# A fused cross-attention, self-attention and gated low-rank layer: all engines' instruction order and the load order redone

## The chip, the cores and the metric

The kernel runs on one NeuronCore of a Trainium2 chip, in one launch. The metric is the time of one execution on the device in microseconds (us); lower is better. PE is TensorE (matrix products and transposes), ACT is ScalarE, DVE is VectorE, POOL is GpSimd, and SP is the engine that here only issues the DMA loads and stores.

## The reference, cut to what matters

```
x: (16, 32, 512)   ctx: (16, 512, 512)          # all float32
q1 = fake_quant(layernorm(x)); q2 = fake_quant(ctx)      # round to 8 bits, scale back
x  = x + q1 @ q2                                         # per batch element
h  = layernorm(x)
q, k, v = h @ wq.T + bq, h @ wk.T + bk, h @ wv.T + bv    # 32 heads of 16 channels
x  = x + softmax over heads(q k^T / 4) v                 # per token: 32x32 scores between heads
h  = layernorm(x)
gate = softmax of the 16 largest of 64 scores (h @ Wq.T @ keys.T)
x  = x + ((h @ A.T) * gate) @ B.T * 2
```

The attention is between the 32 heads of one token, not between tokens. The 512 tokens are the 16 batch elements times 32 rows.

## The kernel before, in words

**Tiles.** The 512 tokens are four tiles of 128 tokens (`TILES` = 4), and each tile holds four batch elements (`BPT` = 4). Each batch element has its own context matrix, 512 by 512 in float32, 1 MiB. The sixteen contexts are called c0 to c15: c0 to c3 belong to tile 0, c4 to c7 to tile 1, c8 to c11 to tile 2, c12 to c15 to tile 3.

**A context's way.** SP loads it into one of four `raw` slots (`load_ctx`, L262 to L269; from c4 on it first waits until the context four before it has been quantised). ACT quantises it to 8 bits in `cu8` (`quantise_ctx`, L408 to L423). POOL, or DVE for c2 and c3, subtracts 128 and writes bfloat16 into `cbf` (`center_ctx`, L330 and L615). PE multiplies it with the tile's quantised rows (`product(t, first, end)`, L970 to L985), whose results lie in `ps1`. c3 is loaded and quantised in two halves.

**A tile's way.** (1) `norm_stats`, `norm_1`, `quantise_x`, `center_q1`, `transpose_q1`, `copy_q1T`. (2) four `product`s, `finish_product`, `transpose_y1`, `residual_1`. `shift_x` adds a row term to x before that. (3) Second norm (`norm_2_stats`, then `norm_2` on DVE for tiles 0 and 1, `apply_norm_2` on ACT for tiles 2 and 3), `transpose_h2`, `copy_h2T`. (4) Three projections with wq, wk, wv (`project_q`, `project_k`, `project_v`; `first` and `second` are the two halves of the contraction), biases added on DVE, `spread_heads` (two long DVE transposes, of q and of k). (5) `scores(t, 0)` and `scores(t, 1)`, 64 small products each; `softmax_shift`, `exp_scores`, `transpose_probs`. `place_v` copies v into a block-diagonal tile with four ACT copies. `context(t)` is 64 more small products. (6) `transpose_context`, `residual_2`, third norm, `transpose_h3`, `router_scores`, `choose_experts`, `exp_gates`, `gates`, `bottleneck` (with wa), `gate_z`, `transpose_zg`, `copy_zgT`, `output` (with wb), `residual_3`, store.

**What sets the order.** Each engine's program is a list of such calls written out by hand, and each engine runs its list strictly in order, with a wait on a semaphore wherever it needs another engine's result. So an instruction that waits holds back everything behind it on its engine. Work of four tiles is interleaved in the lists: products of tile t+1 stand between the projections and the attention of tile t. SP's list is an order too: a load that waits for a slot holds back the loads behind it. c12 and c13 are issued after `scores_done` has reached 3, that is after `scores(1, 0)` (L292), and c14 and c15 after `scores(1, 1)` (L295).

**Fillers.** `keep_busy(3)` (L1170) and `keep_clock_up(n)` (L1176) are matmuls whose results nobody reads; they keep TensorE active in places where it would wait.

**Biases.** The three bias rows are spread over 128 partitions by three matmuls with a matrix of ones (`spread_biases`), copied out by ACT (`copy_bias`).

**Router weights.** `transpose_router_weights`, `combine_router_weights` and ACT's `copy_router_weights` run once, between tile 0's v projection and tile 1's q projection, which reuses their PSUM bank and so waits for that copy.

Of the kernel before, what the change touches and what calls it, by code (L numbers as in the profile page):

```python
# [18 lines left out]
S = Q // 2  # L19
# [12 lines left out]
def build(nc, x, ctx, quant_in, biases_in, wqT, wkT, wvT, aT, bT, wrT, keysT, out):  # L32
# [13 lines left out]
    with ExitStack() as stack:  # L46
# [214 lines left out]
        def _(sp):  # L261
# [31 lines left out]
            load_ctx(3 * BPT)  # L293
            load_ctx(3 * BPT + 1)
            sp.wait_ge(sem_scores_done, 4)  # L295
            load_ctx(3 * BPT + 2)
            load_ctx(3 * BPT + 3)
# [11 lines left out]
        def _(pool):  # L309
# [57 lines left out]
            for padded in (q_sb, k_sb):  # L367
                nc.gpsimd.memset(padded[:, D:], 0.0).then_inc(sem_q_pad, 1)
# [3 lines left out]
            rsqrt(1, 0, sem_ln2_mean, sem_ln2_eps, sem_ln2_rstd)  # L372
            pool.wait_ge(sem_h2_ready, 1)
            center_ctx(BPT)
            center_ctx(BPT + 1)
            finish_norm_1(2)
            finish_norm_1(3)
            center_ctx(BPT + 2)
            center_ctx(BPT + 3)
            rsqrt(1, 1, sem_ln2_mean, sem_ln2_eps, sem_ln2_rstd)  # L380
            pool.wait_ge(sem_h2_ready, 2)
            for n in range(2 * BPT, 3 * BPT):
                center_ctx(n)
            for u in range(1, TILES):
                residual_2(u - 1)
                finish_norm_3(u - 1)
                if u == 2:
                    for n in range(3 * BPT + 1, NB):
                        center_ctx(n)
                if u + 1 < TILES:  # L390
                    finish_norm_2(u + 1)
                if u == 1:
                    center_ctx(3 * BPT)
# [4 lines left out]
        def _(act):  # L398
# [145 lines left out]
            shift_x(2)  # L544
            quantise_x(3)
# [3 lines left out]
            quantise_ctx(3 * BPT)  # L549
            apply_norm_2(2)  # L550
# [3 lines left out]
            copy_zgT(0)  # L554
            copy_h2T(2)
            copy_q1T(3)
            shift_x(3)
            quantise_ctx(3 * BPT + 1)
            quantise_ctx(3 * BPT + 2)
            for u in range(2, TILES):  # L560
                apply_norm_3(u - 1)
                if u == 2:
                    quantise_ctx(3 * BPT + 3)
                copy_h3T(u - 1)
                exp_scores(u, 0)
                place_v(u)
                exp_scores(u, 1)
                exp_gates(u - 1)
                copy_zgT(u - 1)
                if u + 1 < TILES:  # L570
                    apply_norm_2(u + 1)
                    copy_h2T(u + 1)
# [6 lines left out]
        def _(dve):  # L579
# [280 lines left out]
            row_sum_term(1)  # L860
            dve.wait_ge(sem_x_rest_in, 16)
            norm_stats(x_sb[:, 2, :], 0, 2, sem_ln1_stats, sem_ln1_mean)
            norm_stats(x_sb[:, 3, :], 0, 3, sem_ln1_stats, sem_ln1_mean)
            bias_q(0)
            norm_1(2)
            spread_heads(qT, q_sb, sem_q_biased, sem_qT_ready, 0)
            bias_k(0)
            spread_heads(kT, k_sb, sem_k_biased, sem_kT_ready, 0)
            finish_product(1)
            residual_1(1)  # L870
# [3 lines left out]
            bias_v(0)  # L874
            transpose_probs(0, 0)
            center_q1(2)
            row_sum_term(2)
            transpose_v(0)
# [5 lines left out]
            bias_k(1)  # L884
            transpose_context(0)
            spread_heads(kT, k_sb, sem_k_biased, sem_kT_ready, 1)
            finish_product(2)
            norm_3(0)
            softmax_shift(1, 0)
            residual_1(2)  # L890
            norm_2_stats(2)
            bias_v(1)
            transpose_probs(1, 0)
            softmax_shift(1, 1)
            transpose_v(1)
            transpose_probs(1, 1)
            choose_experts(0)
            gates(0)
            gate_z(0)
            sum_gates(0)  # L900
            center_q1(3)
            row_sum_term(3)
# [411 lines left out]
```

## Time and profile before

| | us |
|---|---|
| median of 3 runs | 147.32 |
| lowest and highest of them | 145.54, 147.86 |
| the profiled execution: its own time | 144.67 |
| the span inside it that the profile covers | 142.9 |
| PE busy | 117.8 (82%) |
| DVE busy | 93.5 (65%) |
| ACT busy | 71.2 (50%) |
| POOL busy | 47.1 (33%) |

Everything below counts from the start of the 142.9 us span. The remaining 1.77 us of the execution's own time lie around the span. Busy shares are averages over the whole span; the stages have different limits, so they don't say by themselves what a change is worth. The matmul record's length overlaps with the next one's, so the distance from one start to the next is shorter than the length shown.

### The profile page before, as it was taken

The numbers are of one execution on the slowest core, as the hardware profiler recorded it, in microseconds if no ns is written. First come the engines' busy times: TensorE is split into PE (matmuls) and PEld (weight loads), VectorE is DVE, ScalarE is ACT, GpSimd is POOL, SyncE is SP. The second block draws the span as 40 slices with busy tenths as digits, with TensorE's granted clock in tenths as the row PEclk, the third lists the DMA queues.
The fourth block names the chain that finished last, engine by engine and source line by source line (L and its number), as shares of the span: only waits on it lengthen the run. The fifth ranks groups of instructions, "written<-read, shape, count | busy, mean of one in ns | idle before, by whom it ended". The sixth has DMA issues, their size and how long they took to land.

```text
span 142.9 us, 4282 instructions
## 1 busy us (share of the span) xinstructions
PE 117.8 (82%) x1864; PEld 70.6 (49%) x1864; DVE 93.5 (65%) x189; ACT 71.2 (50%) x87; POOL 47.1 (33%) x61
## 2 busy tenths in 40 slices
PE   0029657992898999989599999999999799899992
PEld 0024343432566447657155445965444376446881
DVE  5740696417579988699582377799347759893512
ACT  0369976559356999038923991372302115411120
POOL 4018225259507553923407575000830000002000
PEclk9999999999999999999999999999999999999999
DMA  2899999999999920079920100000010000000102
GB/s 63 314 421 419 392 406 403 420 403 382 423 420 384 388 81 5 0 310 381 388 108 5 73 2 0 5 5 5 0 73 2 0 5 5 5 0 21 52 5 73
DMA packets 7093, 24.44 MB, mean 171 GB/s; under 512 B 1185, under 2 KB 1441, under 8 KB 5154
## 3 DMA queue, kind: packets, MB, share of 16 engines
q1 hardware_dynamic: 6928, 24.16, 43.3%
q8 instruction: 15, 0.25, 0.7%
q14 instruction: 4, 0.03, 0.1%
q10 hardware_dynamic: 146, 0.01, 0.1%
HBM read 23.11 MB, written 1.05 MB: 169 GB/s over the span
## 4 chain that ended last, share of the span: by engine, by line
PE 55%; DMA 17%; ACT 11%; DVE 8%; issue 5%; POOL 1%; SPq 0%; DVEq 0%; ACTq 0%
PE ps_b L1042 19%; PE ps_a L1042 14%; DMA wv<-in_L_attn_wv_dram 13%; PE ps_att L1111 5%; ACT cu L422 4%; DMA raw<-in_ctx_dram 4%; PE ps L982 3%; PE ps_att L1122 3%; PE ps_att L1145 2%; ACT v_diag L440 2%; PE ps_t L1023 1%; PE ps L1097 1%; DVE v_diag L839 1%; PE ps_b L1164 1%; PE ps_a L1164 1%
## 5 line engine op out<-in xcount | busy, mean ns | idle before, releaser
L422 ACT ACTIVATE cu<-raw,sc_in,sc_recip 128x2048 uint8<-128x2048 f32 x15 | 30.9, 2088 | 6.4 <-DMA raw<-in_ctx_dram 6.3
L336 POOL TENSOR_SCALAR cbf<-cu 128x2048 bf16<-128x2048 uint8 x14 | 26.6, 1903 | 18.6 <-ACT cu L422 16.8
L324 POOL TENSOR_SCALAR var_eps<-mean_var 128x1 f32<-128x1 f32 x12 | 2.7, 223 | 55.8 <-DVE mean_var L583 55.7
L982 PE MATMUL ps<-q1T,cbf 128*128 128x33 bf16 x256 | 7.9, 178 | 4.5 <-POOL cbf L336 2.8
L440 ACT COPY v_diag<-vT 32x512 f32<-32x512 f32 x16 | 10.1, 633 | 2.4 <-DVE vT L704 2.1
L1111 PE MATMUL ps_att<-kT,qT 16*32 16x32 f32 x1024 | 10.5, 193 | 0.9 <-issue 0.7
L982 PEld LDWEIGHTS ps<-q1T,cbf 128*128 128x128 bf16 x256 | 7.3, 96 | 7.3 <-POOL cbf L336 3.5
L447 ACT ACTIVATE probs<-probs 128x512 f32<-128x512 f32 x8 | 5.0, 627 | 11.7 <-DVE probs L712 11.7
L1111 PEld LDWEIGHTS ps_att<-kT,qT 16*32 16x32 f32 x1024 | 9.6, 104 | 1.9 <-issue 1.7
L581 DVE BATCH_NORM_STATS2 stats<-x_sb 128x6 f32<-128x512 f32 x12 | 8.2, 686 | 2.1 <-DMA x_sb<-in_x_dram 1.3
L959 PE MATMUL ps_t<-ident_bf,q 128*128 128x128 bf16 x12 | 1.4, 248 | 10.0 <-DVE q L606 10.0
L459 ACT COPY h3T<-ps_t 128x256 f32<-128x256 f32 x8 | 2.6, 375 | 13.6 <-PE ps_t L1023 13.6
L587 DVE TENSOR_SCALAR h<-x_sb,mean_var,rstd 128x512 f32<-128x512 f32 x7 | 4.9, 693 | 5.9 <-POOL rstd L327 5.8
L696 DVE STREAM_TRANSPOSE qT<-q_sb 128x1024 f32<-128x1024 f32 x4 | 7.8, 1958 | 0.3
L696 DVE STREAM_TRANSPOSE kT<-k_sb 128x1024 f32<-128x1024 f32 x4 | 7.8, 1946 | 0.3
L1042 PE MATMUL ps_b<-wb,zgT 128*128 128x512 f32 x16 | 7.6, 606 | 0.5 <-ACT zgT L459 0.5
L1042 PE MATMUL ps_a<-wq,h2T 128*128 128x512 f32 x16 | 7.4, 602 | 0.7 <-ACT h2T L429 0.7
L1042 PE MATMUL ps_b<-wv,h2T 128*128 128x512 f32 x16 | 7.8, 610 | 0.0
L1042 PE MATMUL ps_a<-wv,h2T 128*128 128x512 f32 x16 | 7.5, 599 | 0.3 <-DMA wv<-in_L_attn_wv_dram 0.3
L327 POOL TENSOR_TENSOR rstd<-var_eps,minus_half 128x1 f32<-128x1 f32 x12 | 7.1, 588 | 1.0
L1042 PE MATMUL ps_a<-wa,h3T 128*128 128x512 f32 x16 | 7.4, 602 | 0.0
L1042 PE MATMUL ps_a<-wk,h2T 128*128 128x512 f32 x16 | 7.3, 595 | 0.0
(135 smaller groups left out, 222.3 us busy)
## 6 DMA issues: line engine op xcount, KB each, us to landing
raw<-in_ctx_dram SPq DMA_DIRECT2D x15, 1024.0 KB, 10.7
raw<-in_ctx_dram SPq DMA_DIRECT2D x2, 512.0 KB, 11.8
wq<-in_L_attn_wq_dram SPq DMA_DIRECT2D x1, 1024.0 KB, 14.0
wk<-in_L_attn_wk_dram SPq DMA_DIRECT2D x1, 1024.0 KB, 12.4
wv<-in_L_attn_wv_dram SPq DMA_DIRECT2D x1, 1024.0 KB, 19.0
wa<-in_L_ffn_A_w_dram SPq DMA_DIRECT2D x1, 1024.0 KB, 13.1
wb<-in_L_ffn_B_w_dram SPq DMA_DIRECT2D x1, 1024.0 KB, 15.5
out_dram<-x_sb SPq DMA_DIRECT2D x3, 256.0 KB, 2.0
```

The source lines that it names most:

```text
L327: nc.gpsimd.tensor_tensor(rstd[:, norm, t:t + 1], var_eps[:, norm, t:t + 1], minus_half[:, :], ALU.pow).then_inc(rstd_sem, 1)
L336: nc.gpsimd.tensor_scalar(cbf[:, n % BF_SLOTS, :, :], cu8[:, n % U8_SLOTS, :], -CENTER, 1.0, ALU.add, ALU.mult).then_inc(sem_ctx_bf_pool, 1)
L422: nc.scalar.activation(cu8[:, n % U8_SLOTS, :], raw[:, n % RAW_SLOTS, :], ACT.Identity, bias=sc_in[:, 3:4], scale=sc_recip[:, 2:3]).then_i ...
L440: nc.scalar.copy(v_diag[rows, :, g, 0:HD], vT[rows, :, :])\
L447: nc.scalar.activation(probs[:, half, :], probs[:, half, :], ACT.Exp, scale=HD ** -0.5).then_inc(sem_s_exp, 1)
L581: nc.vector.bn_stats(stats[:, norm, t, :], src).then_inc(stats_sem, 1)
L587: nc.vector.tensor_scalar(dst, src, mean_var[:, norm, t, 0:1], rstd[:, norm, t:t + 1], ALU.subtract, ALU.mult).then_inc(done_sem, 1)
L696: nc.vector.transpose(dst[:, :, :].rearrange("p i h -> p h i"), view(src[:, :], 0, [[HD, H], [1, Q]])).then_inc(done, 1)
L982: last = nc.tensor.matmul(ps1[:, m // 2, col:col + LW], cbf[:, n % BF_SLOTS, c, m * P:(m + 1) * P], q1T[:, t, c, b, :], start=(c == 0), st ...
L1042: last = nc.tensor.matmul(dst[:, :], aT[:, c, :], w[:, c, :], start=(c == 0), stop=(c == KC - 1))
L1111: last = nc.tensor.matmul(ps_att[Q * j:Q * j + H, i, :], qT[rows, i, :], kT[rows, i, :], start=True, stop=True)
L1122: last = nc.tensor.matmul(view(ps_att[Q * j:Q * (j + 1), 0, :], BPT * H * i, [[1, BPT * (HD + 1)]]), eT[:, token, :], v_diag[:, token, :, ...
```

## The change

It changes no instruction's work but one filler's operands. It changes the order of the calls in the lists of all five engines. In short:

- SP: c4 is issued directly behind c3, ahead of the second tile's x, the rest of x and wq; c5 comes before wk; c11 comes behind wa and wb.
- ACT: `shift_x(0)` moves up behind c0's quantisation, c4's quantisation ahead of the bias copies, `copy_h2T(1)` ahead of `copy_router_weights`, `place_v(0)` ahead of `copy_q1T(2)`, `apply_norm_2(2)` from behind c12's quantisation to behind `copy_zgT(0)`.
- PE: the biases first of all; half of `project_k(0)` behind two products of tile 1; the first product of tile 2 ahead of `context(0)` and the last product of tile 2, `product(2, 3, 4)`, ahead of `project_v(1, first)` instead of behind it; fillers moved.
- DVE and POOL: the same kind of exchanges, written out.

```diff
@@ sync (SP) @@
             load_x(0, 1, sem_x_in)
-            for n in range(BPT):
-                load_ctx(n)
+            load_ctx(0)
+            load_ctx(1)
+            load_ctx(2)
+            load_ctx(3)
+            load_ctx(4)
             load_x(1, 2, sem_x1_in)
+            load_x(2, 4, sem_x_rest_in)
             sp.dma_start(wq[:, :, :], chunked(wqT)).then_inc(sem_wq_in, 16)
-            load_ctx(BPT)
+            load_ctx(5)
             sp.dma_start(wk[:, :, :], chunked(wkT)).then_inc(sem_wk_in, 16)
-            load_x(2, TILES, sem_x_rest_in)
-            load_ctx(BPT + 1)
-            load_ctx(BPT + 2)
-            load_ctx(BPT + 3)
+            load_ctx(6)
+            load_ctx(7)
             sp.dma_start(wv[:, :, :], chunked(wvT)).then_inc(sem_wv_in, 16)
...
-            for n in range(2 * BPT, 3 * BPT):
-                load_ctx(n)
+            load_ctx(8)
+            load_ctx(9)
+            load_ctx(10)
             sp.dma_start(wa[:, :, :], chunked(aT)).then_inc(sem_a_in, 16)
             sp.dma_start(wb[:, :, :], chunked(bT)).then_inc(sem_b_in, 16)
+            load_ctx(11)
             sp.wait_ge(sem_scores_done, 3)
@@ scalar (ACT) @@
             quantise_x(0)
-            for n in range(BPT):
-                quantise_ctx(n)
-            for i in range(3):
-                copy_bias(i)
+            quantise_ctx(0)
             shift_x(0)
+            quantise_ctx(1)
+            quantise_ctx(2)
+            quantise_ctx(3)
+            quantise_ctx(4)
+            copy_bias(0)
+            copy_bias(1)
+            copy_bias(2)
             quantise_x(1)
-            quantise_ctx(BPT)
+            copy_q1T(1)
             copy_h2T(0)
-            copy_q1T(1)
+            quantise_ctx(5)
+            quantise_ctx(6)
+            quantise_ctx(7)
             shift_x(1)
-            for n in range(BPT + 1, 2 * BPT):
-                quantise_ctx(n)
             quantise_x(2)
-            quantise_ctx(2 * BPT)
+            quantise_ctx(8)
             copy_router_rows()
             exp_scores(0, 0)
+            copy_h2T(1)
             copy_router_weights()
-            copy_h2T(1)
-            quantise_ctx(2 * BPT + 1)
-            quantise_ctx(2 * BPT + 2)
+            quantise_ctx(9)
+            quantise_ctx(10)
             exp_scores(0, 1)
+            place_v(0)
             copy_q1T(2)
-            place_v(0)
-            quantise_ctx(2 * BPT + 3)
+            quantise_ctx(11)
+            quantise_x(3)
             shift_x(2)
-            quantise_x(3)
             exp_scores(1, 0)
             apply_norm_3(0)
             copy_h3T(0)
-            quantise_ctx(3 * BPT)
-            apply_norm_2(2)
+            quantise_ctx(12)
             exp_scores(1, 1)
             place_v(1)
             exp_gates(0)
             copy_zgT(0)
+            apply_norm_2(2)
             copy_h2T(2)
...
@@ vector (DVE) @@
             center_ctx(3)
+            finish_product(0)
             dve.wait_ge(sem_x1_in, 16)
             norm_stats(x_sb[:, 1, :], 0, 1, sem_ln1_stats, sem_ln1_mean)
-            finish_product(0)
+            residual_1(0)
             norm_1(1)
-            residual_1(0)
...
             softmax_shift(0, 1)
-            norm_1(3)
-            transpose_probs(0, 1)
             bias_q(1)
             spread_heads(qT, q_sb, sem_q_biased, sem_qT_ready, 1)
+            transpose_probs(0, 1)
...
+            gates(2)
+            sum_gates(2)
+            gate_z(2)
@@ tensor (PE) @@
             def keep_busy(count):
                 for _ in range(count):
-                    nc.tensor.matmul(ps_att[:, S:, :].rearrange("p i h -> p (i h)"), ident[:, :], h1[:, 0, :],
+                    nc.tensor.matmul(ps_att[:, S:, :].rearrange("p i h -> p (i h)"), ones[:, :], bias_rows[:, 0:D],
                                      start=True, stop=True)
...
+            spread_biases()
             transpose_q1(0)
-            spread_biases()
...
             project_k(0, first)
-            project_k(0, second)
             product(1, 0, 1)
             product(1, 1, 2)
+            project_k(0, second)
             product(1, 2, 3)
             project_v(0, first)
             product(1, 3, 4)
...
             project_k(1, second)
+            product(2, 0, 1)
             context(0)
-            product(2, 0, 1)
             product(2, 1, 2)
             product(2, 2, 3)
+            product(2, 3, 4)
             project_v(1, first)
-            product(2, 3, 4)
             scores(1, 0)
...
             transpose_h3(0)
-            keep_clock_up(3)
             router_scores(0)
             bottleneck(0, first)
             bottleneck(0, second)
+            keep_clock_up(3)
             context(1)
...
             product(3, 2, 3)
+            router_scores(1)
             product(3, 3, 4)
-            router_scores(1)
             scores(2, 1)
+            transpose_y1(3)
             bottleneck(1, first)
-            transpose_y1(3)
             bottleneck(1, second)
...
             output(2, first)
+            keep_clock_up(5)
             output(2, second)
-            keep_clock_up(5)
```

## Rows read from the trace of the kernel before

**Rows 1.** The page: the chain that ended last, share of the span by engine.

```profile
PE 55%; DMA 17%; ACT 11%; DVE 8%; issue 5%; POOL 1%; SPq 0%; DVEq 0%; ACTq 0%
```

**Rows 2.** By stretch: length, busy PE, PEld, DVE, ACT, POOL, granted clock, DMA share, GB/s.

```profile
0.00:36.86 36.86, 19.69 (x156) 10.60 (x156) 20.57 (x43) 23.88 (x20) 15.85 (x28) 1.00 0.94 364
36.86:60.08 23.22, 22.55 (x581) 14.28 (x581) 19.09 (x29) 15.17 (x16) 11.83 (x9) 1.00 0.62 241
60.08:73.53 13.45, 11.22 (x231) 7.16 (x231) 10.68 (x27) 8.55 (x14) 4.47 (x8) 1.00 0.78 315
73.53:99.80 26.27, 26.02 (x452) 15.23 (x452) 18.39 (x38) 13.94 (x19) 9.39 (x8) 1.00 0.04 13
```

**Rows 3.** The chain of waits in order of time: start, length, what.

```profile
17.82 19.00 DMA wv<-in_L_attn_wv_dram
...
60.09 5.43 DMA raw<-in_ctx_dram
...
67.55 0.80 ACT h L513
68.35 0.52 ACT probs L447
...
71.42 1.15 PE ps_att L1122 x64
```

**Rows 4.** SP's issues in order of time: start, length, what.

```profile
11.21 0.33 SPq L269 DMA_DIRECT2D raw<-in_ctx_dram  x1
...
37.02 0.51 SPq L291 DMA_DIRECT2D wb<-in_L_ffn_B_w_dram  x1
```

**Rows 5.** Loads by size, us to landing: c3's second half (issued 3.23), then wb.

```profile
raw<-in_ctx_dram SPq DMA_DIRECT2D x1, 512.0 KB, 12.1
...
wb<-in_L_ffn_B_w_dram SPq DMA_DIRECT2D x1, 1024.0 KB, 15.5
```

**Rows 6.** PE's timeline: start, length, what, and what ended the idle time before.

```profile
25.25 3.70 PE L1042 MATMUL ps_a<-wq,h2T 128*128 128x512 f32 x8 [0.68 <-ACT h2T L429]
...
35.96 0.57 PE L982 MATMUL ps<-q1T,cbf 128*128 128x33 bf16 x16 [2.79 <-POOL cbf L336]
...
56.43 1.96 PE L1042 MATMUL ps_b<-wv,h2T 128*128 128x512 f32 x4
58.23 0.56 PE L982 MATMUL ps<-q1T,cbf 128*128 128x33 bf16 x16
58.73 1.33 PE L1111 MATMUL ps_att<-kT,qT 16*32 16x32 f32 x128
```

**Rows 7.** The bias matmuls: duration min/median/max in ns, first and last start.

```profile
L967 PE MATMUL ps_a<-bias_rows,ones x2: 1061/1112/1163, 10.4 to 11.4; 128*128 128x512 f32 x2
...
L967 PE MATMUL ps_att<-bias_rows,ones x2: 593/692/791, 13.9 to 14.5; 128*128 128x512 f32 x2
```

**Rows 8.** ACT's timeline.

```profile
18.75 0.73 ACT L506 ACTIVATE x_sb<-x_sb,row_term 128x512 f32<-128x512 f32 x1
...
45.01 0.37 ACT L476 COPY wr_keys<-ps_b 128x256 f32<-128x256 f32 x1 [0.26 <-PE ps_b L1089]
...
53.79 2.09 ACT L422 ACTIVATE cu<-raw,sc_in,sc_recip 128x2048 uint8<-128x2048 f32 x1
```

**Rows 9.** POOL's timeline.

```profile
55.96 1.90 POOL L336 TENSOR_SCALAR cbf<-cu 128x2048 bf16<-128x2048 uint8 x1 [3.77 <-ACT cu L422]
```

**Rows 10.** DVE's timeline.

```profile
18.07 0.68 DVE L581 BATCH_NORM_STATS2 stats<-x_sb 128x6 f32<-128x512 f32 x1
18.79 0.18 DVE L583 BATCH_NORM_AGGREGATE mean_var<-stats 128x2 f32<-128x6 f32 x1
...
50.72 0.71 DVE L722 STREAM_TRANSPOSE eT<-probs 128x512 f32<-128x512 f32 x1 [0.28 <-ACT probs L447]
51.36 0.65 DVE L672 TENSOR_TENSOR q_sb<-ps_b,biases 128x512 f32<-128x512 f32 x1
52.11 1.95 DVE L696 STREAM_TRANSPOSE qT<-q_sb 128x1024 f32<-128x1024 f32 x1
```

More of the change, by code:

```diff
@@ L372, in _ @@
             rsqrt(1, 0, sem_ln2_mean, sem_ln2_eps, sem_ln2_rstd)
+            finish_norm_1(2)
             pool.wait_ge(sem_h2_ready, 1)
[L374 to L376 removed]
+            center_ctx(4)
+            center_ctx(5)
+            for padded in (q_sb, k_sb):
+                nc.gpsimd.memset(padded[:, D:], 0.0).then_inc(sem_q_pad, 1)
+            center_ctx(6)
+            center_ctx(7)
             finish_norm_1(3)
[L378 to L379 removed]
             rsqrt(1, 1, sem_ln2_mean, sem_ln2_eps, sem_ln2_rstd)
             pool.wait_ge(sem_h2_ready, 2)
[L382 to L393, printed above, removed]
+            center_ctx(8)
+            center_ctx(9)
+            center_ctx(10)
+            center_ctx(11)
+            residual_2(0)
+            finish_norm_3(0)
+            finish_norm_2(2)
+            residual_2(1)
+            center_ctx(12)
+            center_ctx(13)
+            finish_norm_3(1)
+            center_ctx(14)
+            center_ctx(15)
+            finish_norm_2(3)
+            residual_2(2)
+            finish_norm_3(2)
             rsqrt(2, TILES - 1, sem_ln3_mean, sem_ln3_eps, sem_ln3_rstd)
@@ L554, in _ @@
             copy_zgT(0)
+            apply_norm_2(2)
             copy_h2T(2)
+            shift_x(3)
+            quantise_ctx(13)
+            quantise_ctx(14)
             copy_q1T(3)
[L557 to L572, printed above, removed]
+            apply_norm_3(1)
+            quantise_ctx(15)
+            copy_h3T(1)
+            place_v(2)
+            exp_scores(2, 0)
+            exp_scores(2, 1)
+            exp_gates(1)
+            copy_zgT(1)
+            apply_norm_2(3)
+            copy_h2T(3)
+            apply_norm_3(2)
+            copy_h3T(2)
+            exp_scores(3, 0)
+            place_v(3)
+            exp_scores(3, 1)
+            exp_gates(2)
+            copy_zgT(2)
             copy_h3T(TILES - 1)
@@ L899, in _ @@
             gate_z(0)
+            transpose_context(1)
             sum_gates(0)
-            center_q1(3)
-            row_sum_term(3)
-            for u in range(2, TILES):
-                transpose_context(u - 1)
-                residual_3(u - 2)
-                norm_3(u - 1)
-                bias_q(u)
-                spread_heads(qT, q_sb, sem_q_biased, sem_qT_ready, u)
-                bias_k(u)
-                spread_heads(kT, k_sb, sem_k_biased, sem_kT_ready, u)
-                if u + 1 < TILES:
-                    bias_v(u)
-                    softmax_shift(u, 0)
-                else:
-                    softmax_shift(u, 0)
-                    bias_v(u)
-                transpose_v(u)
-                if u + 1 < TILES:
-                    finish_product(u + 1)
-                transpose_probs(u, 0)
-                softmax_shift(u, 1)
-                choose_experts(u - 1)
-                transpose_probs(u, 1)
-                if u + 1 < TILES:
-                    residual_1(u + 1)
-                gates(u - 1)
-                gate_z(u - 1)
-                if u + 1 < TILES:
-                    norm_2_stats(u + 1)
-                sum_gates(u - 1)
+            residual_3(0)
+            norm_3(1)
+            bias_q(2)
+            spread_heads(qT, q_sb, sem_q_biased, sem_qT_ready, 2)
+            bias_k(2)
+            spread_heads(kT, k_sb, sem_k_biased, sem_kT_ready, 2)
+            bias_v(2)
+            transpose_v(2)
+            softmax_shift(2, 0)
+            finish_product(3)
+            transpose_probs(2, 0)
+            softmax_shift(2, 1)
+            choose_experts(1)
+            residual_1(3)
+            gates(1)
+            transpose_probs(2, 1)
+            gate_z(1)
+            norm_2_stats(3)
+            transpose_context(2)
+            sum_gates(1)
+            residual_3(1)
+            norm_3(2)
+            bias_q(3)
+            spread_heads(qT, q_sb, sem_q_biased, sem_qT_ready, 3)
+            bias_k(3)
+            spread_heads(kT, k_sb, sem_k_biased, sem_kT_ready, 3)
+            softmax_shift(3, 0)
+            bias_v(3)
+            transpose_v(3)
+            transpose_probs(3, 0)
+            softmax_shift(3, 1)
+            choose_experts(2)
+            transpose_probs(3, 1)
+            gates(2)
+            sum_gates(2)
+            gate_z(2)
             t = TILES - 1
@@ L1232, in _ @@
             output(0, second)
+            project_q(2, first)
             transpose_q1(3)
-            project_q(2, first)
             project_q(2, second)
```

27 lines of the change are left out of this document (14 added, 13 removed).

## The prediction

> **What bounds the kernel now.** I read the chain of waits first. PE holds 55% of it, DMA 17% [rows 1], so this is a kernel in which PE works nearly all the time, with some places where it waits. The table by stretch shows where. Until 36.86 us PE is busy for only 19.69 us, while the DMA engines are at a share of 0.94 [rows 2]. The chain crosses this stretch on one load: wv, issued at 17.82, lands at 36.82 [rows 3]. What PE does before that has room. From 36.86 to 60.08 PE is busy 22.55 of 23.22 us: PE is the bound. From 60.08 to 73.53 it is busy only 11.22 of 13.45, and from 73.53 to 99.80 again 26.02 of 26.27 [rows 2]. In the weak stretch the chain is: the load of c12, which may only be issued once `scores(1, 0)` is done, 5.43 us to landing, its quantisation on ACT, then on ACT `apply_norm_2(2)` at 67.55, `exp_scores(1, 1)` at 68.35, `place_v(1)`, and only then `context(1)` at 71.42 [rows 3]. So three things set the end: when wv lands, how soon after it `scores(1, 0)` ends, and what stands on ACT between c12 and `place_v(1)`.
>
> **Loads up to wv.** The new order has the same loads ahead of wv: 12 MiB with wv. Nothing is taken out, so wv can only land earlier or later if the queue runs dry or runs at another pace. Dry: c4 waits for c0's quantisation and is issued at 11.21 [rows 4], and now x1, the rest of x and wq stand behind it. At that moment what is queued lasts until c3's second half lands, 3.23 + 12.1 = 15.3 [rows 5], so 4.1 us. A MiB landed 5.43 us after its issue with an idle DMA [rows 3]; its own transfer takes about 2.6 (the six loads behind wv take from 36.82 to wb's landing at 37.02 + 15.5 = 52.5 [rows 3 to 5]), which leaves 2.8 us of delay, less than 4.1. The queue does not run dry. Pace: between 15.3 and 36.82 lie 7.75 MiB, 2.8 us each. At that pace the new order lands c4 at 18.1, x1 at 18.8, wq at 23.0, c5 at 25.8, wk at 28.5, wv at 36.8. I take 0 for wv; the ends are -1.3 (if the 7.75 MiB ran at 2.6) and +1.3 (as much the other way, since no row bounds it).
>
> **Work before 36.86.** `shift_x(0)` ahead of c1 delays the later contexts of tile 0 by its 0.73 us [rows 8], and the statistics of x1, 0.68 + 0.18 [rows 10], now stand between `finish_product(0)` and `residual_1(0)`. At most 1.6 us together: `project_q(0)` goes from 25.25 [rows 6] to 26.85 at the latest, after wq's 23.0. It takes 3.7, the first half of K 1.85 (wk is there), two products 1.14, the second half of K 1.85: 35.4. The next product waited for POOL until 35.96 before [rows 6] and will again. The first half of `project_v` needs wv at 36.82. So the delay is hidden, with 36.82 - 0.57 - 35.4 = 0.8 us to spare; without that cover it would cost its 1.6. c4 earlier, the exchanged K half and the bias copies are worth 0 for the same reason: the load of wv ends last.
>
> **Tile 1 to tile 2: product(2, 3) pulled ahead.** Before, PE went from three products of tile 2 to `project_v(1, first)` at 56.43, then to `product(2, 3)` at 58.23, then `scores(1, 0)` at 58.73 [rows 6]. The product's operand, c11 centred, was ready at 55.96 + 1.90 = 57.86 [rows 9], only 0.37 before PE came for it. The projection was the cover of that work. Now the product stands first: PE comes for it at 56.43 and waits, because PE's queue lets nothing pass. ACT reaches c11 no sooner. Its list up to there holds the same calls (c9, c10, an exp, the four v copies, q1T), and it began c11 at 53.79 [rows 8] without waiting; since `copy_router_weights` (0.37 [rows 8]), which filled a wait for `transpose_h2(1)`, now stands behind that wait, c11 comes 0.37 later: quantised from 54.16, centred at 58.23. PE: product from 58.23, v half from 58.73 for 1.80 (58.23 - 56.43), `scores(1, 0)` from 60.53. **+1.80 us.** Bounds: +1.4 if ACT regains the 0.37, +2.3 if POOL or ACT lose half a microsecond more.
>
> c11's load, now behind wa and wb, lands last of the same six: 52.5, 1.6 us before ACT wants it at 54.16. Cost 0. `copy_h2T(1)` and the router copy still end just before `project_q(1)` needs them, 0 to +0.3.
>
> On DVE, `bias_q(1)` and the long transpose of q now stand ahead of `transpose_probs(0, 1)`: 50.72 + 0.65 + 1.95 + 0.71 [rows 10] = 54.0. `context(0)` stands behind `product(2, 0)` now; with its 1.15 [rows 3] and two products of 0.57 to go until 56.43 it starts near 54.1. Cost 0, with a tenth to spare, +0.3 at most. k's transpose ends sooner and is not late next.
>
> **c12 and place_v(1).** c12 and c13 wait for `scores(1, 0)` and so are issued, and land, 1.80 later (the queue is empty, the 5.43 stay). ACT quantises c12 at once. Then `apply_norm_2(2)` no longer stands ahead of the exp: 68.35 - 67.55 = **-0.80 us** [rows 3] for `place_v(1)`, `context(1)`, `exp_gates(0)`, the gating and `output(0)`. What it does now, behind `copy_zgT(0)`, is needed by `transpose_h2(2)` behind half of `output(0)`, 1.8 us later: 0.80 fits. The filler moved from before the router to the wait before `context(1)` is worth 0, since PE still reaches `context(1)` early.
>
> **From 73.53 on** PE has no gap worth naming until 99.80 [rows 2], and the exchanges keep the sum of each chain: `gates(1)` before `transpose_probs(2, 1)` delays `context(2)` by about half a microsecond, but the second norm of tile 3 (statistics, POOL, ACT) ended last there and has the same work ahead of it. `place_v(2)` ahead of `exp_scores(2, 0)` is covered by `finish_product(3)` on DVE. `residual_2(1)` on POOL now goes ahead of c12 and c13, which are needed only after the scores of tile 2. `sum_gates(2)` before `gate_z(2)` and the fillers between the halves of `output(2)` sit beside `context(3)` and the third norm. 0, with -0.5 and +0.5 as ends.
>
> **Sum:** 1.80 - 0.80 = **+1.0 us**. The profiled execution's own time is 144.67 (span 142.9): 145.7. That execution lay 2.65 us below the median of the runs, 147.32; on the median the sum gives **148.3**. The ends of all terms added give about -0.9 and +3.0 on top of the median.
>
> **Rivals.**
>
> *A. The wait at product(2, 3) does not come* (ACT or POOL get to c11 1.8 us earlier). Only the -0.8 is left: 146.5. For it speaks only that 23 us of ACT's list are reshuffled there; against it, that ACT began c11 without waiting and with only 0.37 us of room. Chance 0.12.
>
> *B. The loads run faster in the new order.* wv lands up to 1.3 earlier and the whole chain shifts: 148.3 - 1.3 = 147.0. For it: 2.8 against 2.6 us per MiB in two parts of the same trace. Against: same bytes and sizes. Chance 0.12, and 0.06 more for a gain beyond 2%, several of these together.
>
> *C. Slower: TensorE turns slow in the front part.* The first bias matmuls took 1061 ns, one of the last 593 [rows 7], the same shape: at first PE runs at half pace (the rows' granted clock says 1.00 [rows 2] and does not show it), after nothing at all. Now the biases run before the first transposes, and PE then waits for c0's centring and has only short bursts of products until the fillers. If PE falls back to half pace, six filler matmuls cost 0.47 each, 2.8 us, and the eight of `project_q(0)` up to 3.8 more. It decides once it exceeds the 0.8 us of room before wv: +2.0 with the fillers alone, 150.3; up to +5.8 with q, 154. Against it: in the old order a gap of 2.79 us before 35.96 was followed by 1.96 us for four wide matmuls, no slower than elsewhere [rows 6]. Chance 0.12.
>
> The Trainium skill, "TensorE: Matmul & The Clock Gate", Part 1, says that the half-rate clock is the default state, that sustained activity releases it, and that an idle stretch brings it back. By that rule an earlier warm-up followed by a wait is wasted, which speaks against moving the biases; the trace agrees in its slow first matmuls (1061 ns), and shows no fall after the gap of 2.79 us.
>
> *D. The loads come later.* wv lands 1.3 late, or c11, last of its six, more than 1.6 late, and the PE chain behind it shifts with the excess; with the stall that makes 3 us or more: 150.3 and over. Only the changed queue speaks for it. Chance 0.08.
>
> *The forecast itself*, +1.0 within about -0.5 and +1.5 around it: chance 0.50.
>
> **How the numbers follow.** About 2% (2.9 us) is what can be told from no change. Forecast, A, B and half of C lie within it: 0.50 + 0.12 + 0.12 + 0.06 = 0.80. Beyond it upward are the other half of C and D, 0.14; downward the 0.06 named under B. The range takes the terms' ends on the median, 146.4 to 150.3, and since the runs before alone went from 145.54 to 147.86, it reaches down to 145.4.
>
> **What would show it.** Right: wv lands at 36.8 give or take 0.5; PE idle about 1.8 us before the 16 small matmuls of `product(2, 3)`, ended by POOL's cbf; `scores(1, 0)` 1.8 later than before; the c12 load again in the chain; no h (`apply_norm_2`) between c12's quantisation and the exp; `context(1)` near 72.4; the end of the span near 143.9. Wrong: PE idle elsewhere between 36.8 and 56, filler matmuls of 1061 ns, or `output(0)` earlier than 73.5.

## The result and the profile after

The changed kernel takes 147.45 us (median of 20 runs, 146.80 to 149.27); the kernel before, run between them, 147.24 (20 runs, 144.32 to 148.84). The comparison of the undisturbed runs gives a ratio of 1.015 [1.011, 1.019]; it is above the ratio of the medians, 1.001, because it compares with the lower part of the runs before. The forecast was 148.3 (145.4 to 150.3), within 2% of no change: both hold.

The profiled execution after: 147.5 us of its own, span 145.7, against 144.67 and 142.9. That is +2.8, where the forecast made it +1.0. From the page of the changed kernel: the engines' busy time, the granted clock of TensorE (PE) in 40 slices (tenths), and the chain's shares.

```profile
PE 122.4 (84%) x1864; PEld 72.4 (50%) x1864; DVE 93.2 (64%) x189; ACT 70.9 (49%) x87; POOL 46.6 (32%) x61
...
PEclk9999956999999999599999999999999999999999
...
PE 50%; DMA 16%; ACT 16%; issue 7%; DVE 7%; POOL 2%; SPq 0%; ACTq 0%; DVEq 0%
```

PE's busy time rose by 4.6 us with the same 1864 matmuls, and the clock row has two dips, at a seventh and at four tenths of the span. The page before shows none (its row is all 9, and its stretches say 1.00 [rows 2]). ACT's share of the chain rose from 11 to 16% [rows 1]. The same stretches as in [rows 2], cut at the same events (wv has landed, c12 is issued behind `scores(1, 0)`, `output(0)` begins, `output(1)` begins):

```profile
0.00:36.94 36.94, 22.43 (x156) 11.73 (x156) 21.54 (x43) 23.74 (x20) 16.07 (x26) 0.91 0.94 365
36.94:63.54 26.60, 24.34 (x581) 14.76 (x581) 18.66 (x31) 15.07 (x16) 12.81 (x13) 0.94 0.53 208
63.54:76.16 12.62, 11.41 (x231) 7.33 (x231) 10.66 (x26) 7.85 (x13) 1.05 (x3) 1.00 0.83 332
76.16:103.17 27.01, 26.11 (x452) 15.34 (x452) 18.22 (x37) 14.64 (x20) 11.88 (x11) 1.00 0.04 14
```

The first stretch is as long as before. The second took 26.60 instead of 23.22, at a mean clock below 1.00: +3.4. The third took 12.62 instead of 13.45: 0.8 is given back. `output(0)` begins at 76.16, before at 73.53: +2.6. `output(1)` is 3.4 later than 99.80: `context(2)` ahead of it begins at 101.01, behind a wait of 0.60 for DVE's transpose of the probabilities, where before it began at 97.76 without one. By the end it is +2.8. The chain after, in order of time (start, length, what; the rows answer to [rows 3]):

```profile
18.43 18.51 DMA wv<-in_L_attn_wv_dram
...
63.55 5.31 DMA raw<-in_ctx_dram
...
74.05 1.16 PE ps_att L1147 x64
```

wv lands at 36.94 (36.82 before); the load of c12 is in the chain again; no h stands between it and probs (ACT's rows are shown further down). PE's timeline after, answering to [rows 6]:

```profile
21.48 4.18 PE L1198 MATMUL ps_att<-bias_rows,ones 128*128 128x512 f32 x6
...
27.04 3.70 PE L1067 MATMUL ps_a<-wq,h2T 128*128 128x512 f32 x8 [0.72 <-ACT h2T L437]
...
36.98 1.98 PE L1067 MATMUL ps_a<-wv,h2T 128*128 128x512 f32 x4 [1.52 <-DMA wv<-in_L_attn_wv_dram]
...
46.83 3.70 PE L1067 MATMUL ps_b<-wq,h2T 128*128 128x512 f32 x8
...
58.33 0.62 PE L1007 MATMUL ps<-q1T,cbf 128*128 128x33 bf16 x16 [1.55 <-POOL cbf L340]
58.79 3.51 PE L1067 MATMUL ps_b<-wv,h2T 128*128 128x512 f32 x4
62.23 0.95 PE L1136 MATMUL ps_att<-kT,qT 16*32 16x32 f32 x90
```

PE stands before `product(2, 3)` for 1.55 us, ended by POOL's cbf, as forecast. What was not forecast is the next row: the same four wide matmuls of `project_v(1, first)` that took 1.96 before [rows 6] take 3.51. PE by stretch (length, busy, granted clock, DMA share, GB/s) tells why:

```profile
54.70:56.80 2.10, 2.08 (x100) 1.00 0.00 0
56.80:58.33 1.53, 0.00 (x0) 1.00 0.00 0
58.33:58.79 0.46, 0.46 (x17) 0.69 0.00 0
58.79:60.50 1.71, 1.71 (x8) 0.50 0.04 10
```

The granted clock is 1.00 through the wait, falls within the 16 small matmuls behind it (0.69 on average) and is 0.50, the level of 1.2 GHz, from 58.79 on. POOL centres c11 from 56.38, as before it did from 55.96 [rows 9]:

```profile
56.38 1.90 POOL L340 TENSOR_SCALAR cbf<-cu 128x2048 bf16<-128x2048 uint8 x1 [3.85 <-ACT cu L430]
```

### The profile page after: what moved, and what is told of

It is laid out like the page before. It is cut to its first block, busy times and chain, and to the rows that moved or that the text cites. A ratio compares the mean times of both kernels' runs of the same rounds, so it can differ in the third digit from the quotient of the medians.

```text
span 145.7 us, 4282 instructions
## 1 busy us (share of the span) xinstructions
PE 122.4 (84%) x1864; PEld 72.4 (50%) x1864; DVE 93.2 (64%) x189; ACT 70.9 (49%) x87; POOL 46.6 (32%) x61
## 3 DMA queue, kind: packets, MB, share of 16 engines
HBM read 23.11 MB, written 1.05 MB: 166 GB/s over the span
## 4 chain that ended last, share of the span: by engine, by line
PE 50%; DMA 16%; ACT 16%; issue 7%; DVE 7%; POOL 2%; SPq 0%; ACTq 0%; DVEq 0%
PE ps_b L1067 17%; DMA wv<-in_L_attn_wv_dram 13%; PE ps_a L1067 12%; ACT cu L430 7%; PE ps_att L1136 4%; DMA raw<-in_ctx_dram 4%; ACT v_diag L448 3%; PE ps_att L1147 3%; PE ps_att L1170 2%; PE ps L1007 2%; PE ps_t L1048 2%; PE ps L1122 1%; POOL cbf L340 1%; DVE v_diag L855 1%; DVE eT L738 1%
## 5 line engine op out<-in xcount | busy, mean ns | idle before, releaser
L1007 PE MATMUL ps<-q1T,cbf 128*128 128x33 bf16 x256 | 8.5, 179 | 4.4 <-POOL cbf L340 2.0
L1067 PE MATMUL ps_b<-wv,h2T 128*128 128x512 f32 x16 | 9.4, 716 | 0.0
L992 PE MATMUL ps_a<-bias_rows,ones 128*128 128x512 f32 x2 | 2.1, 1138 | 8.3 <-DMA bias_rows<-in_biases_dram 8.3
L1067 PE MATMUL ps_b<-wk,h2T 128*128 128x512 f32 x16 | 7.4, 597 | 0.0
L726 DVE TENSOR_REDUCE s_max<-ps_att 128x16 f32<-128x512 f32 x8 | 5.4, 669 | 3.1 <-PE ps_att L1136 3.1
L1067 PE MATMUL ps_b<-wq,h2T 128*128 128x512 f32 x16 | 7.3, 599 | 0.0
```

What stands on the lines that cost most here:

```text
L726: nc.vector.tensor_reduce(s_max[:, half], ps_att[:, half, :], AX_X, ALU.max).then_inc(sem_s_max, 1)
L1007: last = nc.tensor.matmul(ps1[:, m // 2, col:col + LW], cbf[:, n % BF_SLOTS, c, m * P:(m + 1) * P], q1T[:, t, c, b, :], start=(c == 0), st ...
L1067: last = nc.tensor.matmul(dst[:, :], aT[:, c, :], w[:, c, :], start=(c == 0), stop=(c == KC - 1))
```

## The experiments

The question was twofold: what makes the V half slow, and why the medians are nearly equal when the profiled executions differ by 2.8. My theory for the first: the wait itself brings PE to half clock, and without it the V half takes 1.96. Rival: the slowness belongs to the changed order as such and stays without the wait. For the second: the kernel before usually loses in other places what its one profiled execution did not lose.

**The V half put back ahead of the product, in the changed kernel.**

```diff
             product(2, 2, 3)
-            product(2, 3, 4)
             project_v(1, first)
+            product(2, 3, 4)
             scores(1, 0)
```

> The changed kernel with one pair put back: project_v(1, first) ahead of product(2, 3) again. Theory 1 (the product pulled ahead makes PE idle for 1.5 us, and that idle time brings TensorE's clock down to half for the next 3.4 us, which costs another 1.6): both go, the four wide matmuls of project_v(1, first) take 1.96 us instead of 3.51, scores(1, 0) starts near 58.8 instead of 62.2, span 142.1 to 142.7 against 145.7. Rival 1 (the clock falls near 58.8 whatever PE does just before, because of the busy share of the whole stretch or of the front part): only the wait goes, the four matmuls still take about 3.5 us, span 143.9 to 144.2.

Measured: 147.36 (10 runs; the kernel before beside it 146.53, 19 runs), ratio 1.008 [1.003, 1.013]. PE's timeline of it:

```profile
46.65 5.39 PE L1067 MATMUL ps_b<-wq,h2T 128*128 128x512 f32 x8
...
57.98 1.96 PE L1067 MATMUL ps_b<-wv,h2T 128*128 128x512 f32 x4
```

The wait is gone and the V half is at 1.96 again. But `project_q(1)` took 5.39 instead of 3.70, at half clock, and so in part did the router and the bottleneck behind it (1.81 and 4.65 instead of 1.10 and 3.65). So the local part of the theory holds, but the expected span of 142.1 to 142.7 did not come: this execution's was 145.6. The move itself can't have caused the fall at `project_q(1)`, since PE's list is that of the changed kernel up to `product(2, 2, 3)`, which stands behind it, and the changed kernel took 3.70 there. Against the kernel before, the ratio is 0.7% lower than that of the changed kernel (1.015), but the intervals overlap: a gain of the move is not shown.

**The wait filled.** Seven `keep_clock_up` matmuls ahead of the product, everything else as changed.

```diff
             product(2, 2, 3)
+            keep_clock_up(7)
             product(2, 3, 4)
```

> The changed kernel with seven filler matmuls (0.22 us each) ahead of product(2, 3), so that PE waits no longer idle. Theory 1: the wait stays (product(2, 3) still starts near 58.3), but the clock stays at full level and project_v(1, first) takes 1.96 us: span 145.7 - 1.6 = 144.1, at most 144.4. Rival 1: the clock falls all the same, span 145.7 to 145.9.

Measured: 146.99 (4 runs), 1.011 [1.002, 1.021], span 144.6, 0.2 above the highest that was expected.

```profile
47.18 3.70 PE L1067 MATMUL ps_b<-wq,h2T 128*128 128x512 f32 x8
...
56.98 1.81 PE L1204 MATMUL ps<-ident 128*128 128x128 f32 x14
58.68 0.57 PE L1007 MATMUL ps<-q1T,cbf 128*128 128x33 bf16 x16
59.10 1.96 PE L1067 MATMUL ps_b<-wv,h2T 128*128 128x512 f32 x4
```

The order and the product's place in time are those of the changed kernel, only PE is not idle, and the V half takes 1.96 (wv landed 0.35 later in this execution, and all behind it with it). This isolates the cause: the idle time ahead of the product, not the order. It is one profiled execution, but the others agree: over all fourteen kernels of this document, the two with the wait (this change and the next experiment) have these four matmuls at 3.5, the twelve without it at 1.96.

**Only that exchange, in the kernel before.**

```diff
             product(2, 2, 3)
-            project_v(1, first)
             product(2, 3, 4)
+            project_v(1, first)
             scores(1, 0)
```

> The kernel before with one pair exchanged: product(2, 3) ahead of project_v(1, first), nothing else. Theory 1: PE idles 1.4 us before the product, then the half clock: scores(1, 0) near 61.9 to 62.2 instead of 58.7, and without the move of apply_norm_2(2) nothing is given back: span 142.9 + 1.6 + 1.5 = 146.0, 145.7 to 146.4. Rival 1 (the fall needs the rest of the change): 144.3 to 144.7, the wait alone.

Measured: 150.36 (4 runs), 1.019 [1.010, 1.029], span 147.0, above the 146.4 expected.

```profile
58.02 0.58 PE L982 MATMUL ps<-q1T,cbf 128*128 128x33 bf16 x16 [1.16 <-POOL cbf L336]
58.45 3.50 PE L1042 MATMUL ps_b<-wv,h2T 128*128 128x512 f32 x4
61.88 1.38 PE L1111 MATMUL ps_att<-kT,qT 16*32 16x32 f32 x128
```

The exchange alone brings the wait, the half clock and `scores(1, 0)` 3.15 later than 58.73 [rows 6]: 1.5 of wait and late product, 1.6 of clock. The span is longer by 4.1, not 3.15: `context(1)` comes 2.8 later, and the clock falls once more behind its wait of 1.74, so that the first four matmuls of `output(0)` take 3.41 instead of 1.98.

**Only `apply_norm_2(2)` moved, in the kernel before.**

```diff
             quantise_ctx(3 * BPT)
-            apply_norm_2(2)
             exp_scores(1, 1)
...
             copy_zgT(0)
+            apply_norm_2(2)
             copy_h2T(2)
```

> The kernel before with ACT's apply_norm_2(2) moved from behind the quantisation of c12 to behind copy_zgT(0), nothing else. Theory: place_v(1), context(1) and output(0) start 0.8 us earlier: span 142.1. Rival: another wait takes its place (transposed gating on DVE, or transpose_h2(2) waiting for the norm behind output(0, first)), span 142.6 to 142.9.

Measured: 145.57 (10 runs), 0.996 [0.990, 1.002], span 143.5, and the lowest of its spans 142.2. First ACT's timeline of it, then PE's, then the row of the kernel before for the same `context(1)`:

```profile
66.99 2.10 ACT L422 ACTIVATE cu<-raw,sc_in,sc_recip 128x2048 uint8<-128x2048 f32 x1
68.99 0.61 ACT L447 ACTIVATE probs<-probs 128x512 f32<-128x512 f32 x1
```

```profile
20.83 3.75 PE L1173 MATMUL ps_att<-h,ident 128*128 128x512 f32 x6
...
36.08 0.57 PE L982 MATMUL ps<-q1T,cbf 128*128 128x33 bf16 x16 [2.22 <-POOL cbf L336]
36.82 3.51 PE L1042 MATMUL ps_a<-wv,h2T 128*128 128x512 f32 x4 [0.18 <-DMA wv<-in_L_attn_wv_dram]
...
72.15 1.15 PE L1122 MATMUL ps_att<-v_diag,eT 128*32 128x68 f32 x64 [0.75 <-ACT v_diag L440]
```

```profile
71.42 1.15 PE L1122 MATMUL ps_att<-v_diag,eT 128*32 128x68 f32 x64 [1.50 <-ACT v_diag L440]
```

The exp follows the quantisation directly, and the wait before `context(1)` fell from 1.5 to 0.75: the -0.8. But in this execution `project_v(0, first)`, whose place and code are those of the kernel before, took 3.51 instead of 1.98, behind a gap of 2.22 at the place where the kernel before had 2.79. So the gap that did no harm in the profiled execution before does harm in another.

**Only K's second half moved behind two products**, which shortens that gap, in the kernel before.

```diff
             project_k(0, first)
-            project_k(0, second)
             product(1, 0, 1)
             product(1, 1, 2)
+            project_k(0, second)
             product(1, 2, 3)
```

> The kernel before with one pair exchanged on PE: the second half of project_k(0) behind the first two products of tile 1, nothing else. Theory 2 (in most executions of the kernel before, PE's idle 2.2 to 3.0 us ahead of product(1, 2) bring the clock down, and project_v(0, first) behind wv's landing takes 3.51 instead of 1.98; the change closes that gap in part, which is what it gives back): the idle time is cut in two, project_v(0, first) takes 1.98 us, the lowest time stays near 144.5 and the median falls by 0.5 to 1.5 us. Rival 2 (the spread of the kernel before comes from elsewhere): same times as before.

Measured: 145.61 (10 runs; before 147.41, 17 runs), 0.996 [0.989, 1.004].

```profile
36.40 0.57 PE L982 MATMUL ps<-q1T,cbf 128*128 128x33 bf16 x16 [1.05 <-POOL cbf L336]
37.33 1.98 PE L1042 MATMUL ps_a<-wv,h2T 128*128 128x512 f32 x4 [0.36 <-DMA wv<-in_L_attn_wv_dram]
```

The gap is 1.05 and the V half runs at full pace, in the one profiled execution. The median is 1.8 lower, the interval includes no change: alone it is not shown to pay.

**The gap filled instead**, with 22 recorded matmuls more, in the kernel before.

```diff
             product(1, 1, 2)
+            keep_clock_up(11)
             product(1, 2, 3)
```

> The kernel before with eleven filler matmuls ahead of product(1, 2, 3), where PE waits for c6, nothing else. Theory 2: no half clock at project_v(0, first), lowest time as before (144.3 to 144.7), median lower by 1 to 1.5 us (145.1 to 145.6 where the kernel before has 146.5). Rival 2: no change.

Measured: 159.44 (4 runs), 1.090 [1.074, 1.107]. No theory expected that. `project_v(0, first)` is at full pace, but later:

```profile
46.49 1.24 PE L1111 MATMUL ps_att<-kT,qT 16*32 16x32 f32 x122
51.95 0.33 PE L1111 MATMUL ps_att<-kT,qT 16*32 16x32 f32 x6 [4.22 <-issue]
52.20 3.69 PE L1042 MATMUL ps_b<-wq,h2T 128*128 128x512 f32 x4
...
103.28 0.18 PE L1111 MATMUL ps_att<-kT,qT 16*32 16x32 f32 x1 [2.04 <-issue]
...
133.10 0.25 PE L1111 MATMUL ps_att<-kT,qT 16*32 16x32 f32 x5 [2.06 <-issue]
```

PE stops inside a run of identical small matmuls, with no semaphore to wait for, and is at half clock behind the stop (four wide matmuls in 3.69).

**Two more with fillers.** One was the single move of `apply_norm_2(2)` with fillers at three gaps (11, 3 and 3 calls); the other the changed kernel, V half put back (not shown in the cut), with three calls at each of three gaps:

```diff
             project_k(0, second)
+            keep_clock_up(3)
             product(1, 2, 3)
...
             transpose_router_weights()
+            keep_clock_up(3)
             combine_router_weights()
...
             transpose_h3(0)
+            keep_clock_up(3)
             router_scores(0)
```

> The kernel before with apply_norm_2(2) moved behind copy_zgT(0) and fillers where PE waits idle: eleven ahead of product(1, 2, 3), three between the two router weight steps, three ahead of context(1). The sum of what the theories give: span 142.1 without falls on the path, so 143.9 as the usual time with a median at most 144.6, 1.5 to 2.5 us under both kernels. If the fillers only move the falls to other places, as in the run with the v half first: 145.5, as with the moved norm alone.

> The changed kernel with project_v(1, first) ahead of product(2, 3) again and fillers at three places where PE waits (ahead of product(1, 2, 3), between the router weight steps, ahead of router_scores(0)). Theory: the 1.7 us by which the run with the v half first missed its 142.1 to 142.7 came from a half clock at project_q(1, first) (5.39 us for the eight matmuls instead of 3.70); with the fillers it goes: span 142.2 to 142.8, time 144.0 to 144.6. Rival: the changed order of ACT and DVE costs that time itself, span 144 and more with a full clock from 36.8 on.

Measured: 162.9 (6 runs) and 153.9 (4 runs, 1.054). The second one's `project_q(1)`:

```profile
46.81 1.98 PE L1067 MATMUL ps_b<-wq,h2T 128*128 128x512 f32 x4
51.34 1.98 PE L1067 MATMUL ps_b<-wq,h2T 128*128 128x512 f32 x4 [2.54 <-issue]
```

Its clock is full there now, and PE stops all the same. Where it stops differs in the program and agrees in the count. The next rows are from the tables by stretch, up to each kernel's restart, in this order: the gap filled; the norm moved with fillers; and the kernel before, up to 51.90.

```profile
0.00:51.90 51.90, 33.78 (x472) 20.63 (x473) 29.19 (x58) 31.97 (x27) 22.32 (x33) 0.90 0.94 366
```

```profile
0.00:51.45 51.45, 33.09 (x472) 20.84 (x473) 29.20 (x58) 32.08 (x27) 21.93 (x33) 0.93 0.95 368
```

```profile
0.00:51.90 51.90, 34.06 (x472) 19.40 (x473) 33.01 (x63) 33.83 (x31) 23.35 (x33) 1.00 0.94 366
```

Each has done 472 matmuls and 473 weight loads; with the 16 semaphore instructions that the trace records on PE among them, that is 961. The kernel before does them by 51.90 without a stop; a kernel that puts more instructions ahead gets there sooner and has to wait. The later stops stand at fixed counts too. These are the tables up to the last stop of the kernel with the gap filled (133.10) and up to the last one of the changed order with fillers (127.92):

```profile
0.00:132.95 132.95, 106.87 (x1739) 62.43 (x1739) 80.28 (x150) 67.64 (x78) 46.15 (x59) 0.94 0.46 180
```

```profile
0.00:127.80 127.80, 104.16 (x1739) 61.38 (x1739) 80.25 (x150) 67.54 (x78) 45.88 (x59) 0.96 0.49 187
```

Counted with the semaphore instructions, this is 3521, and the stops at 103.28 and, in the other kernel, 98.33 stand at 2753: 10 and 7 times 256 behind 961. Every stop of over 0.8 us without a semaphore, in every run here, stands at 961 or a whole number of times 256 behind it, and PE goes on again, at the later ones as at the first, 1.2 to 1.5 us after a packet of 16 KB of the instruction queue (q8) has ended. In the kernel with the gap filled these packets end at 50.67, 101.90 and 131.72, and PE goes on at 51.95, 103.28 and 133.10. So each stop is the late arrival of a block of 256 instructions. Why a block comes late stays open. Ahead of the first stop the packet begins between 48.9 and 50.7 in every kernel, as the saturated loads drain, also where PE has stood since 47.7; but the packets of the later stops come late with the DMA idle, so the loads can't be the reason there.

**Wide fillers, few instructions.** Three calls of `keep_busy` (6 recorded matmuls, 512 columns each) in place of 22. `keep_busy` has the operands of the changed kernel here and in the run after the next (not shown in the cut).

```diff
             product(1, 1, 2)
+            keep_busy(3)
             product(1, 2, 3)
```

> The kernel before with three wide filler matmuls (12 recorded PE instructions, about 2.6 us) ahead of product(1, 2, 3), in place of the eleven small ones (44 instructions) of the run that took 12 us more. Theory 3 (PE's instructions arrive in blocks; the block that begins behind its 961st recorded instruction is there at 51.9 us in every kernel, and instructions added ahead of it make PE reach that place too early and stand still, again at later blocks): 12 instructions instead of 44 cost little: PE stands still at instruction 961 for 1 to 2.5 us, span 144 to 146. Rival 3 (keeping PE busy in that gap is what hurts, by its traffic or its accumulation bank): about the same loss as with the small ones, span 155 and more.

Measured: 146.7 (10 runs; before 146.84, 23 runs), 1.003 [0.999, 1.006]. The spans lie close together, 144.3 to 146.1. The fillers took 2.82 and overran the gap (`project_v(0, first)` at 37.95 at full pace), and the stop is there in small:

```profile
52.60 0.33 PE L959 MATMUL ps_t<-ident_bf,q 128*128 128x128 bf16 x3 [1.07 <-issue]
```

**Both good moves in the kernel before**: the norm's and K's half.

> The kernel before with two parts of the change alone: apply_norm_2(2) behind copy_zgT(0), and the second half of project_k(0) behind the first two products of tile 1. No instruction is added. Expected if the two add up: 0.8 us under the run with the K half alone (142.7 to 143.2 in span in its undisturbed executions, median time 145.6): lowest span 141.9 to 142.1, median time 144.8, which is under both kernels. Rival (each is worth something only alone): median 145.5 and more.

Measured: **144.32** (6 runs, 143.77 to 145.70), ratio 0.983 [0.977, 0.988]: with the next one, the only version that beats the kernel before clear of the noise. Each of the two moves alone had 0.996 and an interval that includes no change. Its profiled execution still had the half clock once,

```profile
36.92 3.66 PE L1042 MATMUL ps_a<-wv,h2T 128*128 128x512 f32 x4 [0.27 <-DMA wv<-in_L_attn_wv_dram]
```

and was, with 143.9, the longest of its six spans; the others are 142.0 to 142.8.

**The same with one wide filler moved**, from the front to the gap, so that no instruction is added.

```diff
-            keep_busy(3)
+            keep_busy(2)
...
             project_k(0, second)
+            keep_busy(1)
             product(1, 2, 3)
```

> As the kernel with the norm moved and the K half exchanged, and one of the three wide fillers of the front taken to the place ahead of product(1, 2, 3): no instruction added in all. Theory 2 and 3: the rest of the gap ahead of wv is filled without reaching instruction 961 earlier; median 144.8 or up to 0.5 lower. Rival: no difference, or +0.5 and more if the front loses its clock.

Measured: 144.46 (4 runs), 0.983 [0.976, 0.990]. The V half is at 1.98 (37.34), and the time is that of the version without it: no gain on top.

**The biases and the filler's operands put back too**, in the changed kernel with the V half put back (the cut shows the biases alone). The theory tested was that the earlier bias matmuls cause the half clock at `project_q(1)`.

```diff
-            spread_biases()
             transpose_q1(0)
+            spread_biases()
```

> The changed kernel with project_v(1, first) ahead of product(2, 3) again, and in front transpose_q1(0) ahead of spread_biases with the old filler operands. The run with the v half alone put back had spans of 144.1 to 146.2, not the 142.2 of the sum. Theory 4 (the biases up front bring on the extra half-clock stretches, at project_q(1) and later): lowest span 142.1 to 142.7, median time about 145. Rival 4 (they come from the rest of the order, and fall where they fall): lowest span 144 again, median 147.

Measured: 148.9 (10 runs), 1.005 [0.999, 1.010].

```profile
46.77 5.40 PE L1067 MATMUL ps_b<-wq,h2T 128*128 128x512 f32 x8
...
69.40 6.11 PE L1067 MATMUL ps_a<-wa,h3T 128*128 128x512 f32 x8
```

The half clock is at `project_q(1)` and at the bottleneck again, with the old bias order: the earlier bias matmuls are not needed for it, and that theory falls.

## Why the forecast came out as it did

**Loads up to wv: 0.** Right: issued at 18.43, landed at 36.94.

**Work before wv hidden.** Right, and it held more than I had put there. `project_q(0)` began at 27.04, where 26.85 was the latest allowed. The six fillers took 4.18, partly at half clock, instead of 2.74, which is rival C's mechanism and, in part, a sign that the forecast had named as wrong. But it is no mark of the change. Here is their row in the kernel before; with the old bias order they took 3.75 in the kernel with only the norm moved, and 5.15 in the one with only K's half moved.

```profile
20.42 2.74 PE L1173 MATMUL ps_att<-h,ident 128*128 128x512 f32 x6
```

PE still stood 1.52 before wv, where 0.8 of room was forecast. One reading was wrong here: `product(1, 2, 3)` was to wait for POOL until 35.96 again, and it began at 34.90 without a wait, since c6 was centred earlier in the new order and K's second half filled the time. So the slow fillers had no price.

**product(2, 3) pulled ahead: +1.80.** The wait came (1.55, plus 0.3 by which PE and POOL were later), and rival A is out. c11 was quantised from 54.20 (forecast 54.16) and centred at 58.28 (58.23). The step that failed is the next term: "v half from 58.73 for 1.80". It took 3.44 (58.79 to 62.23). The forecast priced the wait as idle time alone; its second price is the half clock on the wide matmuls behind it, +1.6, isolated by the filled wait and by the exchange alone.

**apply_norm_2(2): -0.80.** Right: `context(1)` came 2.63 later where `scores(1, 0)` was 3.50 later, and in the single move its wait fell from 1.50 to 0.75. ACT's timeline after, with the exp and the v copies right behind c12:

```profile
68.89 2.09 ACT L430 ACTIVATE cu<-raw,sc_in,sc_recip 128x2048 uint8<-128x2048 f32 x1 [0.57 <-DMA raw<-in_ctx_dram]
70.89 0.61 ACT L455 ACTIVATE probs<-probs 128x512 f32<-128x512 f32 x1
71.41 2.59 ACT L448 COPY v_diag<-vT 32x512 f32<-32x512 f32 x4
```

**From 73.53 on: 0.** +0.2 from `output(0)` to the end (2.6 to 2.8), within the half microsecond given. The delay of `context(2)` by about half a microsecond came too (0.6) and was regained.

**Sum.** +1.0 was forecast, +2.8 came between the two profiled executions: +1.6 of clock, 0.2 of the rest. On the medians it was +0.2: neither figure is the +1.0, and the time lies in the range partly by luck. I took the profiled execution before for a typical one and only shifted its sum by 2.65. It was not typical: its granted clock was 1.00 throughout, and of the 59 later runs of the same kernel none reached a mean of 1.00; most have 0.976 or 0.965, with spans from 142.7 to 146.8. After has 0.941 to 0.965 in all 20. Of the 59, the 24 at 0.976 have a median span of 144.4 and the 23 at 0.965 one of 146.0: one step of the mean clock goes with 1.6 us, as much as one V half at half clock. At the same mean clock, 0.965, the two have nearly the same spans: 144.6 to 146.8 before, 145.3 to 146.3 after. Both kernels lose to the clock. For before, the place can be shown only in near copies, with the norm moved and with both good moves: 1.5 to 1.7 us at `project_v(0, first)` behind the gap, which the change closes. How often before itself loses there is not known, since only one execution of it has a timeline. The range has a slip as well: the ends of the terms add up to about -1.2 and +3.9, not -0.9 and +3.0; both medians lie inside either.

**My argument against C** was that a gap of 2.79 had been followed by 1.98 us for four wide matmuls. One execution can't carry that. Over the profiled executions, gaps of 2.22 and 1.64 ahead of the last product before wv were followed by the fall, gaps of 3.00, 2.79, 1.05 and 0.78 were not, nor were the waits of 1.52 and 1.53 for wv itself in the changed kernel and in the one with its wait filled.

**Left open.** Why the clock falls at `project_q(1)` in both kernels that have the changed order with the V half put back and nothing added. The order is not enough for it: the changed kernel and the one with its wait filled have the same program on PE up to there and took 3.70 (46.83 and 47.18). Nor did PE wait longer than 0.7 us in the 8 us ahead of the fall. The bias order is excluded. So a fall can come in one execution and not in the next, and one profiled execution of each kernel can't say how often.

## What to carry to other kernels

A wait on the engine that bounds is paid twice: once as idle time and once more on the wide matmuls behind it, if the clock falls; keep the independent projection ahead of the product whose operand is late, and take one execution's clean clock for luck until several agree. Close a gap by moving work into it rather than by adding filler instructions, since these bring the next block of instructions due before it has come. Try the moves of a large reordering singly, and then the good ones together: here two of them, neither of which shows its gain alone, are worth 1.7%, and the whole nothing.

## What the runs showed of the hardware

**The clock falls after some short waits, not after every one, and sometimes without one.** Waits of 1.16 and 1.55 us before `product(2, 3)` were followed by a granted clock of 0.50, which cost 1.6 us on four wide matmuls; at the gap before wv, waits of 2.22 and 1.64 were followed by the fall, one of 3.00 was not; at `project_q(1)` it fell twice with no wait over 0.7 in the 8 us ahead. The Trainium skill, "TensorE: Matmul & The Clock Gate", Part 1, calls the number of matmuls that a kernel runs at the low clock at its start variable from run to run. The fillers of the front agree: 2.74, 2.74 and 3.75 us in three executions whose programs on PE are the same up to there.

**Instructions can come late.** PE stood up to 4.22 us with no semaphore to wait for. All such stops of over 0.8 us stand at a recorded count of 961 or a multiple of 256 behind it, and PE went on 1.2 to 1.5 us after the end of a 16 KB packet of the instruction queue. The Trainium skill, "Runtime: NRT & Kernel Launch", section "Instruction fetch mechanics", says that instructions are refilled in blocks of 16 KiB, or 256 instructions, by a DMA queue, and that the cost of going from one block to the next is mostly hidden. The 16 KB packets and the 256 between the stops agree with the first; the 4.22 us disagree with the second, and 44 instructions more (22 matmuls with their weight loads) took the kernel from 147.4 to 159.4.
